# Routing the second half of the rows before the first expert tile, not between the tiles

## The reference

```
logits = x @ gate_w.T
top_v = jnp.max(logits, axis=-1)
sel = jnp.argmax(logits, axis=-1)
rw = jax.nn.sigmoid(top_v)
for e in range(n_exp):
    mask = (sel == e).astype(x.dtype)
    xs = x * (rw * mask)[:, None]
    g = xs @ w_gate[e].T
    u = xs @ w_up[e].T
    out = out + u * jax.nn.silu(g) @ w_down[e].T
```

## Time and profile before

| | us |
|---|---|
| three timed runs: median (lowest to highest) | 1086.6 (1086.14 to 1090.54) |
| the profiled execution | 1091.98 |
| its span, first to last instruction | 1090.1 |
| POOL busy in the span | 696.2 (64%) |
| DVE busy | 703.9 (65%) |
| PE busy | 964.7 (88%) |
| attention ends (last PE matmul of the logits) | about 978.7 |
| the tiles of the second mixture on PE | 986.6 to 1074.8 |

### The profile page before, as it was taken

One profiled execution on the slowest core, in us unless ns is written; L12 is line 12 of the kernel. 1 busy time (PEld: TensorE's weight loads), 2 busy tenths in 40 slices (PEclk: granted clock), 3 DMA queues, 4 the chain that ended last, 5 costly groups with the idle time before them and its releaser, 6 DMA issues.

```text
span 1090.1 us, 14484 instructions
## 1 busy us (share of the span) xinstructions
PE 964.7 (88%) x5008; PEld 517.9 (48%) x5008; DVE 703.9 (65%) x1139; ACT 475.5 (44%) x766; POOL 696.2 (64%) x396
## 2 busy tenths in 40 slices
PE   6199966989999999999998999999899999876994
PEld 4178732433444454443445444444554444355783
DVE  4845468457688665667776477767656777755662
ACT  4724431534444344444541544444234445525562
POOL 0065340687899917776871677777467788881775
PEclk9589856898999999999999999999999999998997
DMA  9445411043111010000001000000100030014351
GB/s 323 155 128 162 122 55 68 6 141 109 15 15 16 25 49 1 0 2 1 1 1 68 1 1 1 1 2 1 67 2 1 1 116 2 1 68 137 135 148 51
DMA packets 39733, 59.92 MB, mean 55 GB/s; under 512 B 5866, under 2 KB 33518, under 8 KB 38640
## 3 DMA queue, kind: packets, MB, share of 16 engines
q1 hardware_dynamic: 17664, 25.14, 6.9%
q0 software_dynamic: 8736, 17.91, 6.1%
q10 hardware_dynamic: 13264, 15.97, 4.3%
HBM read 27.50 MB, written 25.85 MB: 49 GB/s over the span
## 4 chain that ended last, share of the span: by engine, by line
PE 64%; DVE 15%; POOL 9%; ACT 4%; issue 3%; DMA 2%; ACTq 1%; POOLq 0%; SPq 0%
PE ps_o L1311 16%; PE ps L1298 11%; PE ps L1128 8%; DVE maxes L1134 7%; PE ps L844 6%; POOL arena_b L1779 6%; PE ps_x L1108 5%; DVE rows_store L1678 4%; PE ps L1453 3%; PE ps_x L1332 2%; POOL sorted_x L1019 2%; PE ps L828 2%; ACT rows_store L762 1%; PE ps_x L860 1%; PE ps_o L860 1%
## 5 line engine op out<-in xcount | busy, mean ns | idle before, releaser
L1134 DVE TENSOR_REDUCE maxes<-ps 128x2 f32<-128x1024 f32 x256 | 310.7, 1217 | 196.0 <-PE ps L1128 195.3
L1779 POOL TENSOR_TENSOR arena_b<-arena_b 128x1024 f32<-128x1024 f32 x112 | 272.3, 2437 | 176.4 <-PE ps_o L1311 140.8
L1779 POOL TENSOR_TENSOR arena_b<-arena_b,hot_store 128x1024 f32<-128x1024 f32 x112 | 272.5, 2433 | 68.5 <-PE ps_o L1311 35.3
L1298 PE MATMUL ps<-q_split,keys_now 64*128 64x512 f32 x1536 | 205.0, 392 | 0.0
L1537 ACT ACTIVATE arena_b<-ps 128x1024 f32<-128x1024 f32 x144 | 143.2, 1023 | 101.2 <-PE ps L1298 101.2
L1298 PEld LDWEIGHTS ps<-q_split,keys_now 64*128 64x128 f32 x1536 | 145.4, 186 | 32.7 <-issue 4.1
L1311 PE MATMUL ps_o<-arena_b,latent_now 128*64 128x512 f32 x576 | 148.2, 616 | 1.3 <-ACT arena_b L1537 1.3
L1537 ACT ACTIVATE hot_store<-ps 128x1024 f32<-128x1024 f32 x112 | 111.9, 1022 | 57.5 <-PE ps L1298 57.5
L1311 PE MATMUL ps_o<-hot_store,latent_now 128*64 128x512 f32 x448 | 116.5, 616 | 2.5 <-ACT hot_store L1537 2.5
L1678 DVE RECIPROCAL rows_store<-rows_store 128x256 f32<-128x256 f32 (+1 forms) x72 | 112.6, 1565 | 4.8 <-ACT rows_store L1548 4.8
L1128 PE MATMUL ps<-keys_max_now,q_split 64*128 64x512 f32 x384 | 93.9, 485 | 7.6 <-DVE maxes L1134 6.4
(11 more groups left out here) (323 smaller groups left out, 1140.3 us busy)
## 6 DMA issues: line engine op xcount, KB each, us to landing
sorted_y<-arena_b ACTq DMA_DIRECT2D x40, 128.0 KB, 2.0
x_res<-sorted_x SPq DMA_DIRECT2D x32, 130.0 KB, 3.0
x_res<-x_in SPq DMA_DIRECT2D x4, 1024.0 KB, 13.6
scaled_x<-rows_store SPq DMA_DIRECT2D x16, 256.0 KB, 2.1
keys_now<-keys_next SPq DMA_DIRECT2D x4, 1024.0 KB, 4.6
sorted_x<-blank ACTq DMA_DIRECT2D x2, 1560.0 KB, 13.0
sorted_x<-blank ACTq DMA_DIRECT2D x2, 1430.0 KB, 10.2
arena_a<-w_gu SPq DMA_DIRECT2D x1, 2048.0 KB, 14.4
```

The costliest lines, as they stand in the source:

```text
L1134: nc.vector.tensor_reduce(maxes[:, 2 * m:2 * m + 2], bank[:, :, :], AX_X, ALU.max) \
L1298: last = nc.tensor.matmul(ps_s[n % 2][:, a, :], keys_now[h, key, k], query[h, p, q], start=False, stop=(kt >= KT - STRIDE and query is q_h ...
L1779: nc.gpsimd.tensor_tensor(t, t, prob(k, kt).rearrange("p a n -> p (a n)"), ALU.add) \
```

## The change

The routing of part b leaves the tiles. On DVE its seven steps stand in a row behind the copy of the last logits and ahead of `dve_experts`; on PE `pe_back` and `pe_ranks_late` stand ahead of `pe_experts`; on ACT the exponential stands ahead of `act_experts`. POOL issues the 16 scatters of part b right behind those of part a, and then all 46 result rows. The codes of the later tiles stay between the tiles, now behind tiles 1 and 3 in place of 6 and 7.

```
-                if tag == "f2" and t == 0:
-                    pe_back(pe, BATCH - 1, PAIRS * (BATCH - 1) + 1)
-                if tag == "f2" and t == 2:
-                    pe_ranks_late(pe, "b", NT - AHEAD)
...
-                    if t == 2:
-                        act_exp_top_late(act, "b", AHEAD, NT)
...
-                if t == 0:
-                    dve_scale_late(dve, "b", AHEAD, NT, 1)
-                elif t == 1:
-                    dve_back(dve, BATCH - 1)
-                    dve.wait_ge(sem("logits_back"), BATCH)
-                    dve_one_hot_late(dve, "b", AHEAD, NT)
+                if t == 1:
+                    dve_counts_late(dve, small[:, 5, :], small[:, 6, :])
                 elif t == 3:
-                    dve_weight_late(dve, "b", AHEAD, NT)
-                elif t == 4:
-                    dve_starts_late(dve, "b", *run_b, small[:, 6, :])
-                elif t == 5:
-                    dve_slots_late(dve, "b", AHEAD, NT)
-                elif t == 6:
-                    dve_counts_late(dve, small[:, 5, :], small[:, 6, :])
-                elif t == 7:
                     dve_codes_late(dve)
...
-            for t in range(FIRST_OUT):
-                pool_row_out(pool, t)
             pool.wait_ge(sem("scale_late"), 4)
             pool.wait_ge(sem("slots_late"), 2)
             for t in range(AHEAD, NT):
                 pool_scatter(pool, "b", t)
-            for t in range(FIRST_OUT, SLOT_TILES_2):
+            for t in range(SLOT_TILES_2):
                 pool_row_out(pool, t)
...
             nc.vector.tensor_copy(logit_q[:, :], LATE_LOGITS).then_inc(sem("pair_kept"), 1)
+            dve_scale_late(dve, "b", AHEAD, NT, 1)
+            dve_back(dve, BATCH - 1)
+            dve.wait_ge(sem("logits_back"), BATCH)
+            dve_one_hot_late(dve, "b", AHEAD, NT)
+            dve_weight_late(dve, "b", AHEAD, NT)
+            dve_starts_late(dve, "b", *run_b, small[:, 6, :])
+            dve_slots_late(dve, "b", AHEAD, NT)
             dve_experts(dve, "f2")
...
             act_attention(act)
+            act_exp_top_late(act, "b", AHEAD, NT)
             act_experts(act, "f2")
...
+            pe_back(pe, BATCH - 1, PAIRS * (BATCH - 1) + 1)
+            pe_ranks_late(pe, "b", NT - AHEAD)
             pe_experts(pe, "f2")
```

More of the change, by code:

```diff
@@ L79 @@
 LOADING = 8
-FIRST_OUT = 4
 EARLY_GROUPS = 5
```

## The result

The changed kernel takes 1075.58 us (median of four runs, 1069.79 to 1078.71), the kernel before 1087.33 beside it on the same chip (1086.14 to 1090.54): a ratio of 0.9881, 95% interval [0.9833, 0.9929]. Forecast were 1075.7, between 1072.5 and 1080.5. The profiled execution took 1078.71 us, span 1076.9; forecast were 1081.1 and 1079.2. The kernel before was 0.7 us slower here than in the runs that the forecast started from (1086.6), so the gain is 11.8 us by the medians, with 10.9 forecast.

A forecast was written before the change was run, and what follows sets the result against it. The prediction took POOL's late queue of result rows as the bound, with PE behind it. POOL's last issue would start at 1070.8 in place of 1081.71, 10.9 us off the median 1086.6: 1075.7 us, range 1072.5 to 1080.5.

The forecast's parts named there:

- What bounded before: End of the kernel: POOL's queue of result rows, not arithmetic, sets it; last issue 6.4 us later than its data.
- Routing ahead of tile 0: Before the first tile: routing takes 9.2 us, mostly inside an existing 8.14 us wait, so tile 0 is 1.1 us later.
- Tiles: First to last `gate_up`: 73.1 us of steps plus 1.1, 1.6 and 0.6, so `gate_up(45)` comes at 1065.6, against 1070.88.
- Counts and codes: Two pieces left between early tiles: each makes a step 0.82 us too long, together between 0 and 1.64; 1.64 taken.
- The long first step: First `gate_up` step: stays at 2.71 us in place of 1.62, a loss of 1.09 us.
- the clock: PE's first tiles: the rise to full clock may come 2.6 us later, losing 0 to 1.3 us; 0.6 taken.
- The tail: After `gate_up(45)`: 4.4 us to the last finished row, 0.85 more to POOL's last issue, at 1070.8.
- The signs: Wrong if POOL still issues back to back at the end, `gate_up(0)` is after 991, or ten first steps exceed 21 us.
- Slow routing: Rival, DVE's routing before tile 0: slow integer operations end it 2.9 us later; gain 8.0, 1078.6 us; chance 0.09.
- Scatters against row loads: Rival, DMA engines at the early tiles: part b's scatters slow the loads, some 3 us, 1078.7 us; chance 0.04.
- The low clock: Rival, PE in the tiles: clock stays at half, 3.25 us per tile; ten such tiles give 1091.9 us; chance 0.03.
- POOL as the bound: Rival, POOL's result rows: faster tiles leave POOL's limit of 1067.5, capping the gain at 14.2, 1072.4 us; chance 0.06.

The follow-up runs named there:

- the two later profiles: The changed kernel run twice more with no edit, beside the kernel before: 1074.21 us (ratio 0.9875) and 1075.25 us (ratio 0.9909).

## Why the prediction was right, step by step

**What bounded before.** Right. With the order of before on POOL the gain is 4.5 us in place of 11.1, and the last issue follows POOL's own pace.

**Routing ahead of tile 0.** 9.31 us against 9.2, the ranks' wait 0.77 against 0.6, tile 0 later by 1.0 against 1.1. Three terms, all from windows of before; none off by more than 0.2.

**Tiles.** 76.4 forecast, 74.84, 73.62 and 73.63 measured. Three terms were wrong. The plain steps: 73.1 taken, 72.1 with PE at full clock, as the first four are shorter. Counts and codes: 1.64 taken; behind tiles 1 and 3 the sum is 72.0 and 72.2, behind tiles 10 and 12 it is 71.9, so they cost a few tenths at most (0.9 when they are neighbours). The long first step, 1.09, and the clock, 0.6, were booked as two things, and are one: at a clock of 1.00 the first step is 1.18 us. Together they cost 72.1 to 74.84 or 73.62, so 1.5 to 2.7 us; booked were 1.7, in the middle. The bound on the rise was wrong too: I set T + 15.6 as its latest point and saw T + 16.4.

**The tail.** 5.3 us from `gate_up(45)` to POOL's last issue, measured 1068.48 - 1061.79 = 6.7 in the first profile. The last row was finished when forecast (4.0 + 0.4 against 4.4); POOL was behind again, as the last tiles end faster than its 1.29 us. I had compared POOL's limit with the tiles (3.4 us in hand) for the whole queue and not for its last six rows. This error of +1.4 met the one of -1.6 in the tiles, which is why T + 91.8 lies so near T + 92.0. In the two later profiles it is T + 90.6. Terms off by up to 1.6 us and a sum off by 0.2: that nearness is luck (the two later profiles are off by 1.4), while the sign and the size within about 1.5 us rest on steps that held.

**Close.** 8.4 against 8.4.

**The signs.** One of the three signs of being wrong came true as it was worded: POOL is issuing back to back at the end, for its last six rows. What it was to show, that POOL never catches up, is not so, since POOL idles before most of its rows between 1047.44 and 1062.03. But the picture drawn of the end, POOL idle before its last results and a chain over PE and DVE into the last issue, was wrong: the last issue comes 2.3 us behind the end of DVE's last row (1066.22), and the chain stays on POOL. The other two signs did not come: `gate_up(0)` is at T + 10.3 (991 would be T + 12.2), and the first ten steps take 18.2 us.

**Two slips in the working.** The chances of the cases counted as faster add up to 0.94, not 0.93. And POOL's own limit, 1067.5, keeps the wait for the ranks that the fastest case leaves out; without it the limit would be 1066.9, and the fastest case, 1068.0, would lie 1.1 us above it and not half a us.

**The rivals.** Slow routing: 0.17 us each at lines 637 and 662, where part a had 1.46 and 1.73; dead. Scatters against row loads: the DMA share reached 1.06, PE lost nothing and the issues kept 0.96 us but for one of 1.03; no cost seen. The low clock: it came as a loss of 1.5 to 2.7 us, not of ten tiles. POOL as the bound: not here, but 1.8 to 3.0 us away, and reached once PE is kept at work.

**Left open.** What sets the point at which the clock rises, or makes it fall in one kernel with fillers and not in five others; and why the program ahead of T takes up to 10.5 us more in one profile than in another. Neither was tried by itself.

## What to carry to other kernels

When the end is bound by a queue of issues, ask two things of a change: when its first entry can start, and what stands ahead of it; here each alone gave 4.5 and -2.3 us, both together 11.1. Price an interlude on a side engine by the slack of the tiles around it: alone it was all but free, next to another it cost 0.9 us. And where a part of the program that was not changed differs by more than the effect, measure from a common instruction behind it.

## What the runs showed of the hardware

- PE stood still twice in a full pipeline. After a step 3.3 us too long its granted clock went from 1.00 to 0.87 and 0.50, after one 2.4 us too long it stayed at 1.00 and the steps kept their normal length. One case each.
- With the same PE program the clock rose between 13.5 and 16.4 us behind the same instruction, and the tiles took 74.84 and 73.62 us at the late and the early rise.
- Fillers of 2.3, 2.0 and 1.0 us in the three gaps kept the clock at 1.00 in five profiles of six, with at most 1.48 us idle ahead of the first turns; in the sixth, with 1.80 us, it fell.
- Indirect DMAs of POOL follow one another every 1.26 (scatters) or 1.29 us (result rows). With the DMA engines at a share of 1.0 the scatters kept to 1.26 to 1.29 us, but for one step of 1.34 us in the first profile of the changed kernel.
